# Banded attention and a quantised feed-forward on one core: four score banks in the first half of a batch, and another order of the work around them

## Chip, core and metric

One core of one Trainium2 chip runs the whole program. The metric is the device time of one execution in microseconds; the kernel before took 1425.24 us (median of three). One further execution was taken with the hardware profiler; every duration below is from that one.

## What is computed

Sixteen sequences of 256 tokens with 512 features pass through an attention block against a context of the same shape, and then through a feed-forward block with quantised weights and activations. Cut to what matters:

```
q = rope(layernorm(x) @ wq.T);  k = rope(ctx @ wk.T);  v = ctx @ wv.T      # 16 heads of 32
scores = (q @ k.T) * sqrt(32), only where |query - key| <= 128
attn   = softmax(scores)
x = x + (attn @ v) @ wo.T + wo_b
hidden = gelu(quant16(layernorm(x)) @ quant8(W_in) + b_in)
x = x + quant16(hidden) @ quant8(W_out) + b_out
```

The change lies in the attention block alone.

## The kernel before

**Steps.** The attention block is software-pipelined over the 16 batches. Step b (b = 0 to 15) computes the scores, softmax and weighted sums of batch b, the projections of batch b+1, and what is left of batch b-1 (division by the softmax's denominators, the output projection, the residual). Steps 0 and 1 are written out, steps 2 to 13 are a loop of six rounds with two steps in its body (an even one and an odd one), steps 14 and 15 are written out again. Each engine runs its own list of instructions in the order in which it is written, and waits on semaphores; nothing reorders it. `wait_ge(s, v)` holds an engine, and all that is behind it in its list, until the semaphore has reached v.

**First half of a step.** For each of the 16 heads TensorE (PE) writes a 128x512 block of scores into a PSUM bank (`scores`, L547, two matmuls for a head), and VectorE (DVE) adds the mask and takes the maximum of each row (`row_maxima`, L1002, two instructions for a head). The banks are `ring = bank[0:2]`: head n uses bank n % 2, so head n has to wait until the maxima of head n-2 are taken. After each pair of heads both engines do other work, taken from a table with eight places: `tiles` on PE, `between` on DVE. On PE these are the two tiles of the key projection (`qk_tile(b+1, "k", 0)` and `1`, 24 matmuls each), eight transposes of the normalised x (`x_transposes`, L472), `shares` (below), the two tiles of the query projection, and the two of the value projection (`v_tile`), the second in two pieces. On DVE these are the statistics of the second layernorm (`ln2_moments`, L964 to L984), `invert` (L1044: the reciprocals of the denominators of batch b-1), `largest` (L988), `xt_rest` (L1035: the low part of the transposed x), `rotate` (L1025 to L1028: the rotary embedding, from the banks of the projection), and `normalise` (L1049: batch b-1's weighted sums times the reciprocals).

**How batch b-1's division runs.** The denominators of batch b-1 stand in `den_bank`, which is `q_bank[1]`, at the end of step b-1. `invert` reads them and writes `den_r` (`neg_max` in the rows). `shares` (L482: eight matmuls in the trace with the constant `pick`) spreads the reciprocals over the partitions, into `pv_bank` (banks 6 and 7). `normalise` multiplies. Since x_transposes writes both banks of `q_bank`, it waits for `den_done`, that is, for `invert`. ACT (ScalarE) has by then copied the weighted sums out of `pv_bank` into `oT` (`oT_copy`), so banks 6 and 7 are free from the end of step b-1 on.

**After it.** ACT splits the rotated keys (`split_hi`, L741) and `oT` (`ot_lead`, L772) into high parts, POOL (GpSimd) makes the low parts (L1269, then `ot_rest`, L1280). With these PE starts the second half: the output projection of batch b-1 (`o_products`, L531) is woven into the transposed scores, the exponentials, the weighted sums and the denominators of batch b, and the last matmuls of the step are the transposes of a block of weights (`w_transposes`, L609). The second half uses `ring` with two banks too; the change leaves its order alone.

Of the kernel before, what the change touches and what calls it, by code (L numbers as in the profile page):

```python
# [29 lines left out]
P = 128  # L30
# [50 lines left out]
def build(nc, t):  # L81
# [11 lines left out]
    with ExitStack() as ctx:  # L93
# [90 lines left out]
        ring = bank[0:2]  # L184
        kv_bank = bank[2:4]
# [270 lines left out]
        def _(pe):  # L456
# [7 lines left out]
            def x_transposes(j, s):  # L464

                if s == 0:
                    pe.wait_ge(ln1_norm, 2 * j + 2)
                    wait(pe, wt_done, j - 1)
                    wait(pe, den_done, j - 1)
                    wait(pe, rope_step["q"], ROPE_OPS * j)  # L470
                for c in range(KC):
                    mm = pe.transpose(q_bank[s][:, c * P:(c + 1) * P], x_ln[:, s, c * P:(c + 1) * P], ident[:])  # L472
                mm.then_inc(xt_mm, 1)

            def shares(j):

                for half in range(2):
                    if half == 0:
                        pe.wait_ge(den_done, j + 1)
                    pe.wait_ge(oT_out, 2 * j + half + 1)  # L480
                    for a in range(2):
                        mm = pe.matmul(pv_bank[half][:, a * S:(a + 1) * S], pick[:, 2 * half + a], den_r, start=True, stop=True)  # L482
                    mm.then_inc(share_mm, 1)
# [53 lines left out]
            def scores(b, n):  # L537

                if n % KC == 0:
                    for name in ("k", "q"):  # L540
                        pe.wait_ge(stacked[name][n // KC], STAGED * (b + 1))
                if n < 2:
                    wait(pe, exp_done, H * b)
                else:
                    pe.wait_ge(max_done, 2 * (H * b + n - 1))
                for qb in range(2):
                    mm = pe.matmul(ring[n % 2][:, qb * S:(qb + 1) * S], q_st[0:MROW, n, qb * P:(qb + 1) * P],  # L547
                                   k_st[0:MROW, n], start=True, stop=True)
                mm.then_inc(s_mm, 1)

            def max_transposes(b):

                pe.wait_ge(msplit, 2 * (b + 1))
                wait(pe, onorm, 2 * b)
# [17 lines left out]
            def weighted(b, par, i, kb):  # L572
                if kb == 0:
                    pe.wait_ge(p_ready, 2 * (H * b + KC * (i + 1)))
                    if i == 0:
                        pe.wait_ge(v_done, 2 * (b + 1))
                        wait(pe, onorm, 2 * b)
                    elif i == 2:
                        pe.wait_ge(mT_done, MAX_COPIES * (b + 1))
# [47 lines left out]
            def step(b, par, has_c, has_o, has_proj, has_xt):  # L627

                tiles = [[] for _ in range(H // 2)]
                if has_proj:  # L630
                    tiles[0] += [lambda: qk_tile(b + 1, "k", 0)]
                    tiles[1] += [lambda: x_transposes(b + 1, 0), lambda: x_transposes(b + 1, 1), lambda: qk_tile(b + 1, "k", 1)]
                if has_o:
                    tiles[2] += [lambda: shares(b - 1)]
                if has_proj:
# [325 lines left out]
        def _(dve):  # L961
# [35 lines left out]
            def row_maxima(b, n):  # L997
                dve.wait_ge(s_mm, H * b + n + 1)
                apart(dve)
                for qb in range(2):  # L1000
                    sc = ring[n % 2][:, qb * S:(qb + 1) * S]
# [44 lines left out]
            def normalise(b, half):  # L1046
                dve.wait_ge(share_mm, 2 * b + half + 1)
                part = oT[:, 2 * half:2 * half + 2].rearrange("p i t -> p (i t)")
                dve.tensor_tensor(part, part, pv_bank[half][:], ALU.mult).then_inc(onorm, 1)  # L1049
# [38 lines left out]
            def step(b, par, has_c, has_o, has_proj, has_xt):  # L1088
# [5 lines left out]
                if has_proj:  # L1094
                    between[1] += [lambda: xt_rest(b + 1, 0), lambda: xt_rest(b + 1, 1)]
                    between[2] += [lambda: rotate(b + 1, "k", 0)]
                    between[3] += [lambda: rotate(b + 1, "k", 1)]
                if has_o:
                    between[0] += [lambda: invert(b - 1)]
                    between[4] += [lambda: normalise(b - 1, 0), lambda: normalise(b - 1, 1)]  # L1100
# [299 lines left out]
```

## Time and profile before

| what | us |
|---|---|
| median of three runs | 1425.24 |
| lowest, highest | 1421.88, 1426.4 |
| the profiled execution, its own time | 1428.15 |
| its span | 1426.4 |
| PE busy in the span | 1240.3 (87%) |
| DVE busy in the span | 912.6 (64%) |
| ACT, POOL busy | 692.0 (49%), 454.5 (32%) |

The attention block takes roughly the first 905 us, the feed-forward the rest. Busy shares are means over stages with different limits, so the step must be read in order of time, engine by engine. In the rows a line number such as L547 is the line of the kernel before; "bank<-k_st,q_st" is what an instruction writes and reads; "x4" means that four instructions in a row are merged; what stands in brackets is the time for which the engine stood idle before it, and what ended that.

### The profile page before, as it was taken

What the parts mean: (1) busy time and instruction counts of PE and PEld (TensorE: products, weight loads), DVE (VectorE), ACT (ScalarE), POOL (GpSimd) and SP (SyncE); (2) the same over time, 40 slices, a digit from 0 to 9 for tenths busy, and PEclk for the clock granted to TensorE, in tenths of its full rate; (3) what the DMA queues carried; (4) which work ended last, traced back from release to release, by engine and by line L of the source; (5) the groups of instructions that cost most, each with busy time, mean ns of one, the idle gap of its engine ahead of it and who ended that gap; (6) DMA issues with size and microseconds to landing.
All of it is one profiled execution on the core that took longest, in us unless ns stands there. A gap on an engine that the chain in (4) does not pass through costs nothing.

```text
span 1426.4 us, 26171 instructions
## 1 busy us (share of the span) xinstructions
PE 1240.3 (87%) x7860; PEld 782.0 (55%) x7904; DVE 912.6 (64%) x2359; ACT 692.0 (49%) x1046; POOL 454.5 (32%) x1031
## 2 busy tenths in 40 slices
PE   3689998898898898898898988499999979998888
PEld 3657657657657657657657645344454434433333
DVE  4558558458558468558558654456566658866775
ACT  2243354354354354354354354255556547766664
POOL 2353463463463463463463443100000003111310
PEclk9899999999999999999999997799999989999999
DMA  6432542532542532532532441136555220466664
GB/s 222 119 89 65 145 100 70 143 98 68 144 95 72 142 83 83 144 88 77 144 97 69 115 116 71 66 114 215 196 199 178 83 93 15 139 204 208 192 191 141
DMA packets 88739, 174.54 MB, mean 122 GB/s; under 512 B 12112, under 2 KB 20560, under 8 KB 88656
## 3 DMA queue, kind: packets, MB, share of 16 engines
q1 hardware_dynamic: 74832, 148.45, 35.3%
q10 hardware_dynamic: 13824, 25.17, 6.2%
q8 instruction: 29, 0.48, 0.1%
q14 instruction: 54, 0.44, 0.1%
HBM read 81.30 MB, written 41.94 MB: 86 GB/s over the span
## 4 chain that ended last, share of the span: by engine, by line
PE 36%; issue 27%; DVE 17%; ACT 9%; DMA 7%; POOL 3%; ACTq 1%; DVEq 1%; POOLq 0%; SPq 0%
PE bank L723 7%; DMA h_ring<-hidden_scratch 6%; ACT probs L795 4%; DVE bank L1002 4%; PE bank L568 4%; PE bank L531 4%; PE bank L460 4%; PE bank L461 3%; PE bank L462 3%; PE bank L595 3%; PE bank L582 3%; PE bank L547 3%; ACT q_st L788 2%; DVE row_max L1002 2%; DVE neg_max L1044 2%
## 5 line engine op out<-in xcount | busy, mean ns | idle before, releaser
L1002 DVE CUSTOM_DVE_ANT_0 bank<-bank,mask 128x256 f32<-128x256 f32 x512 | 201.8, 457 | 131.2 <-PE bank L547 100.3
L723 PE MATMUL bank<-wout_int,g_hi 128*128 128x512 bf16 x491 | 186.9, 381 | 24.9 <-DVE g_lo L1247 23.1
L723 PE MATMUL bank<-wout_int,g_lo 128*128 128x512 bf16 x512 | 195.0, 381 | 5.8 <-DVE g_lo L1247 3.0
L692 PE MATMUL bank<-qT_lo,win_int 128*128 128x512 bf16 x512 | 194.0, 379 | 2.8 <-DVE qT_lo L1165 1.6
L692 PE MATMUL bank<-qT_hi,win_int 128*128 128x512 bf16 x489 | 185.4, 379 | 0.0
L795 ACT ACTIVATE probs<-bank 128x512 f32<-128x512 f32 x256 | 144.4, 597 | 61.5 <-PE bank L595 39.7
L568 PE MATMUL bank<-q_st,k_st 128*128 128x256 f32 x512 | 124.2, 326 | 31.2 <-ACT probs L795 24.4
L568 PEld LDWEIGHTS bank<-q_st,k_st 128*128 128x128 f32 x512 | 80.3, 192 | 117.0 <-issue 42.2
L1247 DVE TENSOR_TENSOR g_lo<-h_int,g_hi 128x512 f16<-128x512 f32 x128 | 102.5, 800 | 60.0 <-ACT g_hi L927 58.1
L1305 POOL TENSOR_SCALAR_AFFINE_SELECT probs<-probs 128x128 f32<-128x128 f32 x256 | 82.3, 322 | 150.1 <-ACT probs L795 141.2
L547 PE MATMUL bank<-k_st,q_st 96*128 96x256 f32 x512 | 105.5, 312 | 26.7 <-DVE row_max L1002 14.4
L892 ACT ACTIVATE h_ring<-bank,b_in,g_scale 128x512 f32<-128x512 f32 x96 | 73.5, 780 | 75.1 <-PE bank L692 61.5
L936 ACT ACTIVATE h_int<-h_ring,magic_c,tiny 128x512 f32<-128x512 f32 x96 | 78.4, 817 | 54.9 <-DMA h_ring<-hidden_scratch 44.7
L547 PEld LDWEIGHTS bank<-k_st,q_st 96*128 96x128 f32 x512 | 79.0, 196 | 44.8 <-DVE row_max L1002 23.9
L723 PEld LDWEIGHTS bank<-wout_int,g_hi 128*128 128x128 f16 x512 | 50.2, 98 | 96.8 <-issue 25.8
L1189 DVE TENSOR_REDUCE hmax<-h_ring 128x512 f32 (+1 forms) x96 | 63.4, 683 | 60.5 <-ACT h_ring L892 58.5
L1365 POOL TENSOR_TENSOR xq<-xq,b_out 128x512 f32<-128x512 f32 x32 | 47.0, 1498 | 172.0 <-DMA xq<-x_scratch 164.7
L741 ACT CAST k_hi<-roped 128x1024 fp32r<-128x1024 f32 x16 | 16.8, 1051 | 173.9 <-DVE roped L1028 173.9
L988 DVE TENSOR_REDUCE dmax<-rt 128x512 f32 (+1 forms) x32 | 21.9, 685 | 120.7 <-ACT rt L783 120.7
L582 PE MATMUL bank<-probs,v_sb 128*32 128x256 f32 x1024 | 79.4, 393 | 15.2 <-POOL probs L1307 15.0
L1269 POOL TENSOR_TENSOR k_lo<-roped,k_hi 128x256 fp32r<-128x256 f32 x64 | 45.2, 739 | 145.6 <-ACT k_hi L741 145.6
L1285 POOL TENSOR_TENSOR x_res<-x_res,wo_b 128x512 f32<-128x512 f32 x32 | 40.3, 1280 | 149.4 <-DMA x_res<-in_x 149.4
(146 smaller groups left out, 2948.9 us busy)
## 6 DMA issues: line engine op xcount, KB each, us to landing
hidden_scratch<-h_ring SPq DMA_DIRECT2D x96, 256.0 KB, 2.1
h_ring<-hidden_scratch ACTq DMA_DIRECT2D x96, 256.0 KB, 2.9
k_st<-k_hi SPq DMA_DIRECT2D x128, 128.0 KB, 2.9
q_st<-q_hi SPq DMA_DIRECT2D x128, 128.0 KB, 2.5
xq<-x_scratch SPq DMA_DIRECT2D x16, 1024.0 KB, 6.5
x_ln<-in_x SPq DMA_DIRECT2D x16, 512.0 KB, 3.6
ctx_raw<-in_ctxT SPq DMA_DIRECT2D x16, 512.0 KB, 5.4
k_st<-k_lo SPq DMA_DIRECT2D x64, 128.0 KB, 2.4
```

Source lines behind the costliest of these rows:

```text
L547: mm = pe.matmul(ring[n % 2][:, qb * S:(qb + 1) * S], q_st[0:MROW, n, qb * P:(qb + 1) * P], k_st[0:MROW, n], start=True, stop=True)
L568: mm = pe.matmul(ring[n % 2][:, kb * S:(kb + 1) * S], k_st[:, n, kb * P:(kb + 1) * P], q_st[:, n], start=True, stop=True)
L582: mm = pe.matmul(pv_bank[i // 2][DK * c:DK * (c + 1), (i % 2) * S:(i % 2 + 1) * S], v_sb[:, par, kb, n], probs[:, n % SLOTS, kb], start=kb ...
L692: mm = pe.matmul(bank[f % 4][:], win_int[:, c, f * P:(f + 1) * P], part[:, par, c], start=c == 0 and part is qT_hi, stop=c == KC - 1 and p ...
L723: mm = pe.matmul(bank[4 * par + u][:], part[:, f % 4, u * P:(u + 1) * P], wout_int[:, f], start=f == 0 and part is g_hi, stop=f == FC - 1 ...
L795: act.activation(probs[:, n % SLOTS].rearrange("p k q -> p (k q)"), ring[n % 2][:], ACT.Exp, scale=SCORE_SCALE).then_inc(exp_done, 1)
L892: act.activation(dst, bank[f % 4][:], ACT.Gelu, bias=b_in[:, f:f + 1], scale=g_scale[:, f:f + 1]).then_inc(gelu_done, 1)
L936: act.activation(h_int[:, f % 4], chunk, ACT.Identity, bias=magic_c[:], scale=tiny[:, 5:6]).then_inc(hint_done, 1)
L1002: dve.tensor_tensor_reduce(sc, sc, mask[:, (1 - qb) * P:(1 - qb) * P + S], 1.0, NEG, ALU.add, ALU.max, row_max[:, qb, n:n + 1]).then_inc(m ...
L1189: dve.tensor_reduce(hmax[:, bass.ds(FC * n + f, 1)], src, AX_X, ALU.max, apply_absolute_value=True).then_inc(hmax_done, 1)
L1247: dve.tensor_tensor(g_lo[:, f % 4], h_int[:, f % 4], g_hi[:, f % 4], ALU.subtract).then_inc(glo_done, 1)
L1305: pool.affine_select(out=lower, in_=lower, compare_op=ALU.is_ge, fill=0.0, base=0, pattern=[[-1, P]], channel_multiplier=1).then_inc(p_rea ...
```

## The change

In the first half of a step the scores go through four banks, `ring4 = [bank 0, 1, 6, 7]`: head n uses bank `ring4[n % 4]` and, from head 4 on, waits for the maxima of head n-4 where it waited for those of n-2. Banks 6 and 7 were where `shares` wrote, so `shares` now writes into `q_bank` (banks 4 and 5). There the transposes of x are written too, so these now wait for `normalise` (`onorm`), where they waited for `invert` and the copy of the weights. `shares` stands ahead of the transposes, after heads 2 and 3. The transposes and the second key tile stand one place later, after heads 4 and 5. On DVE `invert` is the first thing in a step, `normalise` comes after head 3, and `xt_rest` and both rotations of the keys stand one place later each.

```diff
+        ring4 = [bank[0], bank[1], bank[6], bank[7]]
...
                 if s == 0:
                     pe.wait_ge(ln1_norm, 2 * j + 2)
-                    wait(pe, wt_done, j - 1)
-                    wait(pe, den_done, j - 1)
+                    wait(pe, onorm, 2 * (j - 1))
                     wait(pe, rope_step["q"], ROPE_OPS * j)
...
             def shares(j):
 
+                pe.wait_ge(wt_done, j + 1)
+                pe.wait_ge(den_done, j + 1)
                 for half in range(2):
-                    if half == 0:
-                        pe.wait_ge(den_done, j + 1)
-                    pe.wait_ge(oT_out, 2 * j + half + 1)
                     for a in range(2):
-                        mm = pe.matmul(pv_bank[half][:, a * S:(a + 1) * S], pick[:, 2 * half + a], den_r, start=True, stop=True)
+                        mm = pe.matmul(q_bank[half][:, a * S:(a + 1) * S], pick[:, 2 * half + a], den_r, start=True, stop=True)
...
+                elif n < 4:
+                    wait(pe, oT_out, 2 * (b - 1) + n - 1)
                 else:
-                    pe.wait_ge(max_done, 2 * (H * b + n - 1))
+                    pe.wait_ge(max_done, 2 * (H * b + n - 3))
...
+                if has_o:
+                    tiles[1] += [lambda: shares(b - 1)]
                 if has_proj:
                     tiles[0] += [lambda: qk_tile(b + 1, "k", 0)]
-                    tiles[1] += [lambda: x_transposes(b + 1, 0), lambda: x_transposes(b + 1, 1), lambda: qk_tile(b + 1, "k", 1)]
-                if has_o:
-                    tiles[2] += [lambda: shares(b - 1)]
-                if has_proj:
+                    tiles[2] += [lambda: x_transposes(b + 1, 0), lambda: x_transposes(b + 1, 1), lambda: qk_tile(b + 1, "k", 1)]
...
             def normalise(b, half):
                 dve.wait_ge(share_mm, 2 * b + half + 1)
+                dve.wait_ge(oT_out, 2 * b + half + 1)
...
-                    between[1] += [lambda: xt_rest(b + 1, 0), lambda: xt_rest(b + 1, 1)]
-                    between[2] += [lambda: rotate(b + 1, "k", 0)]
-                    between[3] += [lambda: rotate(b + 1, "k", 1)]
+                    between[2] += [lambda: xt_rest(b + 1, 0), lambda: xt_rest(b + 1, 1)]
+                    between[3] += [lambda: rotate(b + 1, "k", 0)]
+                    between[4] += [lambda: rotate(b + 1, "k", 1)]
                 if has_o:
-                    between[0] += [lambda: invert(b - 1)]
-                    between[4] += [lambda: normalise(b - 1, 0), lambda: normalise(b - 1, 1)]
+                    between[1] += [lambda: normalise(b - 1, 0), lambda: normalise(b - 1, 1)]
+                    invert(b - 1)
```

Two waits are gone with it: `max_transposes` and the first weighted sums no longer wait for `onorm`.

The first place is PE's list in step 1, from the scores of heads 2 and 3 on (the other odd steps have the same order). Before:

```order
357 L547 MATMUL bank<-k_st,q_st 128x256 [waits max_done]
358 L547 MATMUL bank<-k_st,q_st 128x256
359 L547 MATMUL bank<-k_st,q_st 128x256 [waits max_done]
360 L547 MATMUL bank<-k_st,q_st 128x256
361 L472 MATMUL bank<-ident,x_ln 128x128 [waits den_done,rope_q_step,wt_done,ln1_norm]
362 L472 MATMUL bank<-ident,x_ln 128x128 x7
```

And of the kernel changed, from the same scores on (`neg_max` holds the reciprocals, L481 is `shares`):

```order
354 L548 MATMUL bank<-k_st,q_st 128x256 [waits oT_out]
355 L548 MATMUL bank<-k_st,q_st 128x256
356 L548 MATMUL bank<-k_st,q_st 128x256 [waits oT_out]
357 L548 MATMUL bank<-k_st,q_st 128x256
358 L481 MATMUL bank<-neg_max,pick 128x256 [waits den_done,wt_done]
359 L481 MATMUL bank<-neg_max,pick 128x256 x3
360 L548 MATMUL bank<-k_st,q_st 128x256 [waits max_done,q_stacked1,k_stacked1]
361 L548 MATMUL bank<-k_st,q_st 128x256
362 L548 MATMUL bank<-k_st,q_st 128x256 [waits max_done]
363 L548 MATMUL bank<-k_st,q_st 128x256
364 L472 MATMUL bank<-ident,x_ln 128x128 [waits rope_q_step,onorm,ln1_norm]
365 L472 MATMUL bank<-ident,x_ln 128x128 x7
```

`shares` and the scores of heads 4 and 5 have moved ahead of the transposes, and the transposes wait for `onorm` in place of `den_done`.

The second place is DVE's list in the even step of the loop, from the loop's turn to what PE's transposes wait for. Before, that is the reciprocal:

```order
230 L244 ISA
231 L1002 ISA bank,row_max<-bank,mask 128x256
...
240 L981 ISA
241 L964 BN_STATS bn<-x_res 128x6
...
246 L984 COPY ln_mv<-mv 128x2
...
249 L254 ISA
250 L1044 RECIPROCAL neg_max<-bank 128x256
```

In the kernel changed, it is the second of the two multiplications by the reciprocals (L1048; rows 233 to 242 and 251 to 260 are the maxima of heads 0, 1 and 2, 3):

```order
231 L255 ISA
232 L1042 RECIPROCAL neg_max<-bank 128x256
233 L996 ISA
...
244 L962 BN_STATS bn<-x_res 128x6
...
249 L982 COPY ln_mv<-mv 128x2
...
262 L986 TENSOR_REDUCE dmax<-rt 128x1
263 L1045 REGISTER_ALU
264 L1048 TENSOR_TENSOR oT<-oT,bank 128x512
265 L1045 REGISTER_ALU
266 L1048 TENSOR_TENSOR oT<-oT,bank 128x512
```

Between the start of DVE's step and the release of the transposes there stood the maxima of two heads, the statistics and the reciprocal; now there stand the reciprocal, the maxima of four heads, the statistics, `largest` and both multiplications.

## Rows read from the trace of the kernel before

**Rows 1.** The page's first line: the span of the profiled execution.

```profile
span 1426.4 us, 26171 instructions
```

**Rows 2.** Waits of PE, 55 to 850 us: us in total, times, longest.

```profile
PE bank L472 <- DVE neg_max L1044: 30.1, 13, 4.2
...
PE bank L547 <- DVE row_max L1002: 6.7, 29, 0.9
```

**Rows 3.** PE in step 9: start, us, engine, line, operation, count [idle before].

```profile
534.88 0.40 PE L609 MATMUL bank<-ident_b,w_q 128*128 128x128 bf16 x4
535.08 0.72 PE L547 MATMUL bank<-k_st,q_st 96*128 96x256 f32 x4
...
538.47 0.64 PE L547 MATMUL bank<-k_st,q_st 96*128 96x256 f32 x4
540.64 1.06 PE L472 MATMUL bank<-ident,x_ln 128*128 128x128 f32 x8 [1.54 <-DVE neg_max L1044]
...
544.37 0.64 PE L547 MATMUL bank<-k_st,q_st 96*128 96x256 f32 x4
544.85 1.89 PE L482 MATMUL bank<-neg_max,pick 128*128 128x256 f32 x8
...
554.22 0.50 PE L547 MATMUL bank<-k_st,q_st 96*128 96x256 f32 x2 [0.20 <-DVE row_max L1002]
...
561.39 0.39 PE L531 MATMUL bank<-wo_hi,t_hi 128*128 128x512 f32 x1
```

**Rows 4.** DVE in step 9, the same columns.

```profile
535.76 0.43 DVE L1002 CUSTOM_DVE_ANT_0 bank<-bank,mask 128x256 f32<-128x256 f32 x1 [2.70 <-PE bank L547]
...
537.25 0.69 DVE L964 BATCH_NORM_STATS2 bn<-x_res 128x6 f32<-128x512 f32 x1
...
538.63 1.76 DVE L1044 RECIPROCAL neg_max<-bank 128x256 f32<-128x256 f32 x1
540.31 0.41 DVE L1002 CUSTOM_DVE_ANT_0 bank<-bank,mask 128x256 f32<-128x256 f32 x1
...
541.78 0.69 DVE L988 TENSOR_REDUCE dmax<-rt 128x512 f32 x1
...
544.96 0.43 DVE L1002 CUSTOM_DVE_ANT_0 bank<-bank,mask 128x256 f32<-128x256 f32 x1 [1.30 <-PE bank L547]
...
551.56 0.69 DVE L1028 TENSOR_TENSOR roped<-rt 128x512 f32<-128x512 f32 x1
...
554.02 1.28 DVE L1049 TENSOR_TENSOR oT<-oT,bank 128x512 f32<-128x512 f32 x2
```

**Rows 5.** POOL in step 9, the low parts of the weighted sums.

```profile
556.40 2.54 POOL L1280 TENSOR_TENSOR t_lo<-oT,t_hi 128x512 fp32r<-128x512 f32 x2
```

**Rows 6.** PE in step 10, which follows the loop's turn.

```profile
586.12 0.40 PE L609 MATMUL bank<-ident_b,w_q 128*128 128x128 bf16 x4
...
594.21 1.41 PE L472 MATMUL bank<-ident,x_ln 128*128 128x128 f32 x8 [3.24 <-DVE neg_max L1044]
```

**Rows 7.** DVE in step 10.

```profile
588.78 0.43 DVE L1002 CUSTOM_DVE_ANT_0 bank<-bank,mask 128x256 f32<-128x256 f32 x1 [4.47 <-issue]
...
592.22 1.76 DVE L1044 RECIPROCAL neg_max<-bank 128x256 f32<-128x256 f32 x1 [0.59 <-DVE ln_mv L984]
```

**Rows 8.** PE in steps 2 and 4: transposes, then the first of `shares`.

```profile
164.50 1.76 PE L472 MATMUL bank<-ident,x_ln 128*128 128x128 f32 x8 [2.09 <-DVE neg_max L1044]
...
170.30 1.89 PE L482 MATMUL bank<-neg_max,pick 128*128 128x256 f32 x8
...
271.43 1.97 PE L472 MATMUL bank<-ident,x_ln 128*128 128x128 f32 x8 [3.24 <-DVE neg_max L1044]
...
278.38 0.81 PE L482 MATMUL bank<-neg_max,pick 128*128 128x256 f32 x3
```

**Rows 9.** Stretches: us; busy PE, PEld, DVE, ACT, POOL; granted clock; DMA.

```profile
164.40:166.00 1.60, 1.50 (x9) 1.51 (x9) 1.60 (x9) 0.56 (x1) 0.00 (x0) 0.61 0.00 0
...
540.00:542.00 2.00, 1.35 (x12) 1.39 (x13) 2.00 (x10) 0.69 (x2) 0.00 (x0) 1.00 0.10 39
```

More of the change, by code:

```diff
@@ L543, in scores @@
                     wait(pe, exp_done, H * b)
+                elif n < 4:
+                    wait(pe, oT_out, 2 * (b - 1) + n - 1)
                 else:
-                    pe.wait_ge(max_done, 2 * (H * b + n - 1))
+                    pe.wait_ge(max_done, 2 * (H * b + n - 3))
                 for qb in range(2):
-                    mm = pe.matmul(ring[n % 2][:, qb * S:(qb + 1) * S], q_st[0:MROW, n, qb * P:(qb + 1) * P],
+                    mm = pe.matmul(ring4[n % 4][:, qb * S:(qb + 1) * S], q_st[0:MROW, n, qb * P:(qb + 1) * P],
                                    k_st[0:MROW, n], start=True, stop=True)
@@ L553, in max_transposes @@
                 pe.wait_ge(msplit, 2 * (b + 1))
-                wait(pe, onorm, 2 * b)
                 for qb in range(2):
@@ L576, in weighted @@
                         pe.wait_ge(v_done, 2 * (b + 1))
-                        wait(pe, onorm, 2 * b)
                     elif i == 2:
@@ L1000, in row_maxima @@
                 for qb in range(2):
-                    sc = ring[n % 2][:, qb * S:(qb + 1) * S]
+                    sc = ring4[n % 4][:, qb * S:(qb + 1) * S]
                     dve.tensor_tensor_reduce(sc, sc, mask[:, (1 - qb) * P:(1 - qb) * P + S], 1.0, NEG, ALU.add, ALU.max,
@@ L1047, in normalise @@
                 dve.wait_ge(share_mm, 2 * b + half + 1)
+                dve.wait_ge(oT_out, 2 * b + half + 1)
                 part = oT[:, 2 * half:2 * half + 2].rearrange("p i t -> p (i t)")
-                dve.tensor_tensor(part, part, pv_bank[half][:], ALU.mult).then_inc(onorm, 1)
+                dve.tensor_tensor(part, part, q_bank[half][:], ALU.mult).then_inc(onorm, 1)
             def quantise_win(b):
```

## Prediction

> **What bounds the kernel now.** The span is 1426.4 us [rows 1]; all that the change touches is the attention block, so I read first which waits PE has between 55 and 850 us. Two belong to the first half of a step: the transposes of x wait 30.1 us in all, 13 times, for the reciprocals, and the scores wait 6.7 us, 29 times, for row maxima whose bank they need [rows 2]. So the two-bank ring, which the change doubles, costs little, and the place to look at is what the transposes wait for. Then I read one step in order of time. I call w the start of the weight transposes that end the step before. In step 9, w is 534.88; the transposes start at 540.64 (w + 5.76) after 1.54 us idle, and the output projection, with which the second half opens, at 561.39, 20.75 us behind the transposes [rows 3]. In between PE waits for little (0.20 us before head 11 is such a wait). The even steps of the loop differ in one thing: DVE shows 4.47 us of idle with no releaser before its first maximum, which starts at 588.78, and PE's transposes start at 594.21, that is w + 8.09 [rows 6, 7]. The question is therefore what the change does to two distances: from w to the transposes, and from the transposes to the output projection.
>
> **From w to the transposes, odd steps.** They now wait for the second multiplication (`normalise`), and on DVE there stand ahead of it, each from its start to the next start in [rows 4]: the reciprocal 1.68 (538.63 to 540.31), the maxima of heads 0, 1 1.49 (535.76 to 537.25), the statistics 1.38 (537.25 to 538.63), the maxima of heads 2, 3 1.47 (540.31 to 541.78), `largest` 0.6 (0.69, less some 0.1 by which starts overlap), the multiplications 1.28. That is 7.9. The reciprocal can start when the last denominators are written, which I put at w + 0.2, since PE issues the next scores at 535.08, right behind the weight transposes. From a reciprocal's end (540.39) to the transposes (540.64) it is 0.25. Sum: w + 8.35 where it was w + 5.76, so **2.6 later**. PE's own work does not reach so far: heads 2, 3 are out at w + 4.1 (538.47 and 0.5 for two heads), `shares` adds 1.54 (544.85 until head 6 at 546.39 by the merged group), heads 4, 5 another 0.5: ready at w + 6.1, idle for **2.2 us**. The reciprocals are there by w + 1.9, so `shares` itself waits for nothing; its old cover, the time after the transposes, is given back below.
>
> **From w to the transposes, even steps in the loop (4 to 12, five of them).** The reciprocal now is what DVE has first after the loop's turn. I let it start where the maximum started, at w + 2.66 [rows 6, 7], and add 7.9 and 0.25: w + 10.8, against 8.09, **2.7 later**. In step 10 the statistics took some 0.5 longer than in step 9 (592.22 - 590.28 against 1.38: the first is the reciprocal's start, the second the end of the maxima by the 1.49 above [rows 7]); part of that may stay, so 2.7 to 3.3. `shares` waits here until w + 4.3 or so for the reciprocals, ahead of a longer idle time, at no cost.
>
> **From the transposes to the output projection.** Gone from this stretch are `shares`, heads 4 and 5, and ring waits: 1.54 + 0.5 + some 0.6. New is a wait at the value tile. PE: transposes and second key tile 3.73 (540.64 to 544.37), then twice two heads and a 24-matmul query tile, 3.39 each at most (535.08 to 538.47), then heads 10, 11 for 0.5: ready at 11.0. The value tile overwrites a bank that the second rotation of the keys reads, and this rotation now comes after head 9. DVE: first maximum of head 6 0.59 behind its scores (544.37 to 544.96), so at 4.3; from there two rounds of maxima and rotation are 7.29 (544.96 to 551.56 + 0.69 [rows 4]): 11.6, with the release 11.8. So PE stands 0.8 us there. From the value tile to the output projection it was 561.39 - 554.45 = 6.9 [rows 3], of which 0.2 is a ring wait: 11.8 + 6.7 = **18.5, 2.25 less than 20.75**. POOL runs to the same end: its low parts ended at 558.94, 6.7 behind the rotation's end at 552.25 [rows 4, 5], so now at 18.3 to 18.4. That leaves it 0.1 us of slack where it had 2.4.
>
> **Sum without the clock.** Odd steps 3 to 13 and step 14, which has no turn of the loop ahead of it: 2.6 - 2.25 = +0.35, seven times, 2.5. Even steps: 2.7 to 3.3 less 2.25, +0.6, five times, 3. In steps 0 and 1 some or none of batch b-1's work is there, in step 2 it all is but DVE's late start is not, in step 15 there are no transposes: within 1 us together, by the same counting. **About +5 us.** The four banks let PE run ahead, but what it runs up against is DVE's list, and that list got longer ahead of the release by the maxima of two heads, `largest` and both multiplications.
>
> **The clock.** In step 9, with 1.54 us idle ahead of the transposes, the granted clock is 1.00 (2.4 GHz); in step 2, with 2.09 idle, the stretch from the transposes on shows 0.61 (between 2.4 and 1.2 GHz) [rows 8, 9]. From the transposes to `shares` it took 5.80 us there against 4.21 in step 9 [rows 3, 8], 1.6 more; in step 4, after 3.24 idle, 6.95, 2.7 more [rows 8]. So a fall costs 1.6 to 2.7, and the even steps pay it already. With 2.2 us idle the odd ones are on step 2's side of the two rows: I take six of seven falling at 1.9 (nearer to the low end, where the idle time is nearest): **+11**. Bounds are 0 (none falls) and 19 (seven at 2.7).
>
> Together +16 on a span of 1426.4. The profiled execution took 1428.15 itself, 2.9 above the median of 1425.24; the difference carries over, so the forecast for the median is 1425.2 + 16 = **1441 us**.
>
> The Trainium skill (Perfetto Trace Analysis, Optimizing Tensor Performance, Matmuls) says that independent groups of matmuls should go round through different PSUM banks so that one's evacuation overlaps the next's matmuls. The trace agrees that such waits exist, but prices them at 6.7 us in all [rows 2].
>
> **The rivals.**
> (1) The same chain, but the clock holds in the odd steps, because PE does `shares` and two more heads right before it goes idle. For it: six idle times of 1.54 did no harm. Against: 2.09 did. It gives 1425.2 + 5 = 1430.
> (2) Faster: the 4.47 us of DVE at the loop's turn [rows 7] is not the turn but a delay of the first maximum's own wait. Then the reciprocal starts at w + 0.2 there too, 2.5 sooner than I put it; five times 2.5 is 12.5, and the even steps become odd ones: 1430 - 12.5 = 1417, if the odd ones keep their clock. It decides from the point at which the reciprocal starts before w + 1.5 in steps 4, 6, ... 12. Against it: step 10 and step 9 run the same instructions there, and only the one behind the turn has the idle time.
> (3) The banks pay what the rings cost and the longer list costs nothing, since it runs under PE's run-ahead: 6.7 less, 1418.5. For it, there are 2.25 us per step given back; against, my count of DVE's list, which is 2.6 us longer. The rule of the Trainium skill above would give this one.
> (4) POOL's 0.1 us of slack is not there, and the output projection waits for the low parts of the weighted sums in every step: with 1 us each, 14 more, 1455.
>
> **How the numbers follow.** Forecast with the clock falling in most odd steps 0.57; (1) 0.22; (2) 0.06; (3) 0.05; (4) 0.08; the rest 0.02. The forecast's own bounds are 1435 to 1449 (three to seven falls, low or high price). With (1) it takes in 0.79 from 1427 on, which is the range, opened to 1450. A measurement of this kernel can tell about 0.3%, 4.3 us, from no change. The forecast and (4) are slower by more than that; (1) lies on the border at 1430 and is halved; (2) and (3) are faster. With the rest split: slower 0.76, same 0.13, faster 0.11.
>
> **What would show it.** In the profile after: PE's transposes idle for some 2.2 us in odd and 4 to 5 us in even steps, put down to the multiplication and no longer to the reciprocal; waits of scores for row maxima near zero; a new wait of the value tile for the rotation of 0.8 us; PE's clock in the row of slices lower over the attention block. Wrong would be the whole sum if the transposes started before w + 7.5 in odd steps, the turn's part if the reciprocal started before w + 1.5 in even ones, and the clock's part if transposes to second key tile take 3.7 us in odd steps. The feed-forward must not move.

## The result, and the profile after

| what | before | changed |
|---|---|---|
| median, us | 1422.08 (8 runs) | 1431.47 (8 runs) |
| lowest, highest | 1413.74, 1426.4 | 1430.08, 1437.84 |
| profiled execution, its own time | 1428.15 | 1430.19 |
| its span | 1426.4 | 1428.4 |

The ratio is 1.0081, with a 95% interval of 1.0052 to 1.0109: the change costs 0.8%, 9 to 12 us. On two other chips, where both kernels ran side by side later, it was 1.0038 (1.0011 to 1.0065) and 1.0037 (1.0014 to 1.006), so 0.4 to 0.8% is the size. The change is slower, as forecast, by less than the 16 us of the forecast. The kernel before came out 3.2 us lower over eight executions than over the three from which the forecast of 1441 started.

The waits of PE over the attention block in the changed kernel, which answer to [rows 2]:

```profile
PE bank L568 <- ACT probs L793: 24.3, 45, 1.2
PE bank L472 <- DVE oT L1048: 22.7, 6, 4.2
PE bank L581 <- POOL probs L1306: 15.7, 27, 2.2
PE bank L472 <- issue: 14.1, 8, 1.9
PE bank L548 <- DMA q_st<-q_lo: 10.8, 1, 10.8
PE bank L461 <- DVE roped L1026: 10.5, 15, 0.7
```

The wait for the reciprocals is gone and one for the multiplications (L1048) has come. The trace names it in the even steps; in the odd ones it says "issue", 14.1 us in 8 places, the wait being at the same instruction. Together that is 36.8 us where it was 30.1. The value tile's wait for the rotation of the keys (L1026) is new, 10.5 us in 15 places. The scores' waits for row maxima, 6.7 us before, stand in no row of this list any more. So what the four banks were to remove is gone, and more has come. The feed-forward did not move: from the last weight transposes on it takes 531.4 us, where it took 531.8.

Step 11 of the changed kernel, PE, from w = 641.33 on, the undisturbed odd step (it answers to [rows 3]):

```profile
641.33 0.40 PE L608 MATMUL bank<-ident_b,w_q 128*128 128x128 bf16 x4
641.53 0.72 PE L548 MATMUL bank<-k_st,q_st 96*128 96x256 f32 x4
...
645.39 1.89 PE L481 MATMUL bank<-neg_max,pick 128*128 128x256 f32 x8
...
649.69 1.06 PE L472 MATMUL bank<-ident,x_ln 128*128 128x128 f32 x8 [1.94 <-issue]
...
653.42 0.64 PE L548 MATMUL bank<-k_st,q_st 96*128 96x256 f32 x4
...
661.38 0.50 PE L461 MATMUL bank<-wv_hi,cT_hi 128*128 128x512 f32 x1 [0.72 <-DVE roped L1026]
...
668.21 0.50 PE L530 MATMUL bank<-wo_hi,t_hi 128*128 128x512 f32 x1
```

Transposes at w + 8.36, 1.94 us idle ahead of them; the value tile (L461 with `wv_hi`) waits 0.72; the output projection starts at 668.21, 18.52 behind the transposes. DVE in the same step, which answers to [rows 4]:

```profile
641.46 1.76 DVE L1042 RECIPROCAL neg_max<-bank 128x256 f32<-128x256 f32 x1 [1.95 <-PE bank L594]
643.14 0.41 DVE L1000 CUSTOM_DVE_ANT_0 bank<-bank,mask 128x256 f32<-128x256 f32 x1
...
648.31 1.28 DVE L1048 TENSOR_TENSOR oT<-oT,bank 128x512 f32<-128x512 f32 x2
...
660.63 0.69 DVE L1026 TENSOR_TENSOR roped<-rt 128x512 f32<-128x512 f32 x1
```

The reciprocal starts at w + 0.13; the multiplications start at 648.31 and, 1.38 later, the transposes start. In step 10, the even one, the same places are (PE, then DVE; [rows 6, 7]):

```profile
585.69 0.40 PE L608 MATMUL bank<-ident_b,w_q 128*128 128x128 bf16 x4
...
596.40 1.70 PE L472 MATMUL bank<-ident,x_ln 128*128 128x128 f32 x8 [4.17 <-DVE oT L1048]
```

```profile
587.88 1.76 DVE L1042 RECIPROCAL neg_max<-bank 128x256 f32<-128x256 f32 x1 [4.01 <-issue]
```

w + 10.71 with 4.17 us idle, and the 4.01 us without a releaser at the loop's turn now stand before the reciprocal.

The granted clock, in the columns of [rows 9], in step 9 (transposes at 540.81, which is w + 8.36 too, and 1.94 idle too) and in step 11 (649.69):

```profile
540.80:542.80 2.00, 1.99 (x15) 2.00 (x16) 2.00 (x10) 1.07 (x2) 0.77 (x1) 0.83 0.31 121
542.80:544.80 2.00, 2.00 (x11) 2.00 (x10) 0.60 (x1) 0.00 (x0) 1.75 (x2) 0.50 0.79 260
649.70:651.70 2.00, 2.00 (x18) 2.00 (x19) 2.00 (x10) 1.08 (x2) 0.51 (x1) 1.00 0.45 174
```

Two steps that are alike up to the transposes: in one the clock falls within the first 2 us and then stands at 0.50, that is 1.2 GHz, in the other it holds at 2.4 GHz. From the transposes to the first query tile it is 5.73 us in the one and 4.20 in the other.

### The profile page after: what moved, and what is told of

The parts are those of the page before. It is cut to its first block, busy times and chain, and to the rows that moved or that the text cites. A ratio compares the mean times of both kernels' runs of the same rounds, so it can differ in the third digit from the quotient of the medians.

```text
span 1428.4 us, 26187 instructions
## 1 busy us (share of the span) xinstructions
PE 1229.6 (86%) x7860; PEld 776.5 (54%) x7904; DVE 916.9 (64%) x2359; ACT 688.8 (48%) x1046; POOL 454.9 (32%) x1031
## 4 chain that ended last, share of the span: by engine, by line
PE 39%; issue 28%; DVE 14%; ACT 8%; DMA 7%; POOL 2%; ACTq 1%; DVEq 1%; POOLq 0%; SPq 0%
DMA h_ring<-hidden_scratch 6%; PE bank L721 6%; PE bank L568 4%; PE bank L461 4%; ACT probs L793 4%; PE bank L462 4%; PE bank L463 4%; PE bank L530 4%; PE bank L594 3%; PE bank L581 3%; DVE bank L1000 3%; PE bank L548 3%; ACT q_st L786 2%; DVE roped L1026 2%; PE bank L472 2%
## 5 line engine op out<-in xcount | busy, mean ns | idle before, releaser
L721 PEld LDWEIGHTS bank<-wout_int,g_hi 128*128 128x128 f16 x512 | 50.2, 98 | 96.8 <-issue 21.1
L548 PE MATMUL bank<-k_st,q_st 96*128 96x256 f32 x512 | 89.8, 298 | 14.4 <-DMA q_st<-q_lo 10.8
L461 PE MATMUL bank<-cT_hi,wk_hi 128*128 128x256 f32 x256 | 80.1, 313 | 7.7 <-DVE wk_lo L1074 7.7
```

The lines of the kernel that those rows point to most:

```text
L461: pe.matmul(out, l_hi, r_hi, start=first, stop=False)
L548: mm = pe.matmul(ring4[n % 4][:, qb * S:(qb + 1) * S], q_st[0:MROW, n, qb * P:(qb + 1) * P], k_st[0:MROW, n], start=True, stop=True)
L721: mm = pe.matmul(bank[4 * par + u][:], part[:, f % 4, u * P:(u + 1) * P], wout_int[:, f], start=f == 0 and part is g_hi, stop=f == FC - 1 ...
```

## The experiments

Each kernel but e7 was timed in 5 to 12 executions, beside the kernel before on the same chip. Group 1 ran on one chip; of group 2, e5, e6, e7 and e9 ran on a second, e8 and e10 on a third, e11 and e12 on a fourth. The changed kernel itself was timed beside e10 and e11 alone, so other comparisons with it go by the ratios to the kernel before. "w" is the start of the weight transposes, as ahead. A "fall" is counted where from the transposes to the first query tile it takes 1.3 us or more longer than in an undisturbed step: 4.2 in the changed order, 6.4 in the order of the kernel before, where `shares` and two more heads lie in between; "odd steps" are 3 to 13 and 14, seven in all, "even" ones 4 to 12, five in all.

### Group 1: what the transposes wait for

**e1_invert_first.** The kernel before, with one line moved:

```diff
                 if has_o:
-                    between[0] += [lambda: invert(b - 1)]
                     between[4] += [lambda: normalise(b - 1, 0), lambda: normalise(b - 1, 1)]
+                if has_o:
+                    invert(b - 1)
                 for n in range(H):
                     row_maxima(b, n)
```

> The kernel before with one part of the change alone: the reciprocal of batch b-1's denominators is the first thing VectorE does in a step; two score banks, shares in banks 6 and 7, and PE's order stay. Theory (what PE's transposes wait for decides, not the score banks): the reciprocals are there at w + 1.9 in odd steps (0.2 + 1.7), before PE gets to the transposes, so these start at w + 4.1 where it was w + 5.76, 1.65 less in steps 3 to 14 that are odd or 14; in the even steps of the loop they start at w + 4.5 where it was 8.1 to 9.4, and the clock no longer falls. There VectorE is late by its turn of the loop and gives part back as waits for row maxima: 3.5 to 4 less per step. Sum 7 x 1.65 + 6 x 3.8 = 34 us less than before, about 1388. Rival (VectorE's list bounds the first half, so what is moved in it comes back as waits of scores and tiles for it): under 12 us less.

Measured: 1394.88 us, ratio to before 0.9831 (0.9799 to 0.9864), 24 us less. The transposes start at w + 4.07 in odd steps and w + 4.9 to 6.6 in even ones, with no wait, and no step shows a fall. But 24 us is between the two theories. One reason is in its waits:

```profile
PE bank L547 <- DVE row_max L1002: 24.5, 55, 1.8
```

The scores now wait 24.5 us for row maxima: once the long wait is gone, the two banks do bind, and the output projection comes at w + 25.0 to 25.9 in odd steps and not at w + 24.9. The seven odd steps together save 7.7 us where 11.6 were forecast. The even ones save 4.0 each in the profiled execution, as forecast, and its span is 37 us below that of the first profile of the kernel before; but this execution, 1390.76, was the second fastest of six that go up to 1402.2, and what the slower ones lost no trace shows. The transposes' wait for the reciprocals was worth a lot; the banks are what is late next.

**e2_largest_late, e3_norm_first, e4_largest_twice.** The changed kernel with VectorE's list ahead of the multiplications 0.6 us shorter, shorter by the statistics too, and 0.6 us longer.

```diff
# e2
-                    between[1] += [lambda: largest(b - 2, 1)]
+                    between[2] += [lambda: largest(b - 2, 1)]
# e3, besides e2's
-                    between[0] += [lambda: ln2_moments(b - 2, 1)]
...
                     between[1] += [lambda: normalise(b - 1, 0), lambda: normalise(b - 1, 1)]
+                    if has_c:
+                        between[1] += [lambda: ln2_moments(b - 2, 1)]
# e4, in largest(j, 1), ahead of the reduction
+                    dve.tensor_reduce(tiny[:, 7:8], rt[:, s].rearrange("p c t -> p (c t)"), AX_X, ALU.max,
+                                      apply_absolute_value=True)
```

> The changed kernel with one VectorE instruction moved: the absolute maximum of the second layernorm's input (largest, 0.6 us) stands behind the maxima of heads 4 and 5 and no longer ahead of the two multiplications. Theory (the length of VectorE's list ahead of the release): transposes at w + 7.76 in odd steps, idle before them 1.35 us, clock falls in none of them; 0.6 less in 13 steps and two falls of 1.5 less: 11 us less than the changed kernel. Rival (the list length does not matter, the price of the change is the new wait of the value tile for the keys' rotation, 0.7 us a step): no difference, the transposes' earlier start comes back as a longer wait there.

> The changed kernel with the second layernorm's statistics moved behind the two multiplications and its absolute maximum behind the maxima of heads 4 and 5. Theory: the multiplications now wait for shares and follow the maxima of heads 2 and 3 at once; transposes at w + 7.2 in odd steps and w + 8.4 in even ones (10.2 to 11.4 in the changed kernel), idle 0.8 and 2.0. VectorE reaches the rest of the transposed x 0.5 later relative to the transposes, so a query tile waits 0.5. Sum 7 x 0.7 + 6 x 2 + 3 for two falls of the clock: 20 us less than the changed kernel. Rival (the value tile's wait for the rotation sets the end): no more than e2 gives.

> The changed kernel with the absolute maximum ahead of the multiplications done twice (0.6 us more; the first result goes to an unused cell). Theory: transposes at w + 8.96 in odd steps, idle 2.5; each of 13 steps 0.6 longer, and the clock falls in the odd steps that kept it too (five more at 1.5 to 2.7): 16 to 21 us more than the changed kernel. If the clock does not follow the idle time: 8 us more.

| kernel | median, us | ratio to before | transposes, odd steps | idle before them | falls, odd | falls, even |
|---|---|---|---|---|---|---|
| e3 | 1399.06 | 0.9861 (0.9835 to 0.9887) | w + 7.07 | 0.64 | 0 | 0 |
| e2 | 1417.74 | 0.9969 (0.9943 to 0.9994) | w + 7.77 | 1.35 | 0 of 7 | 5 of 5 |
| changed | 1431.47 | 1.0081 (1.0052 to 1.0109) | w + 8.36 | 1.94 | 2 of 7 | 5 of 5 |
| e4 | 1444.47 | 1.0168 (1.0141 to 1.0195) | w + 8.96 | 2.53 | 3 of 7 | 5 of 5 |

The rows of the transposes in an odd step of e3, e2 and e4 (step 11 in each; w is 616.73, 637.46 and 654.14), one fence for each:

```profile
623.80 1.06 PE L472 MATMUL bank<-ident,x_ln 128*128 128x128 f32 x8 [0.64 <-issue]
```

```profile
645.23 1.06 PE L472 MATMUL bank<-ident,x_ln 128*128 128x128 f32 x8 [1.35 <-issue]
```

```profile
663.10 1.06 PE L472 MATMUL bank<-ident,x_ln 128*128 128x128 f32 x8 [2.53 <-issue]
```

(The row "changed" was timed on another chip.) In e2 and e4 the start of the transposes follows the length of VectorE's list to 0.1 us, in both directions, and the time follows the start. In e3 it follows it only in part: the list is 1.4 us shorter than e2's, the start comes 0.7 earlier. VectorE now stands idle for TensorE's scores of head 2 ahead of the multiplications:

```profile
620.92 0.43 DVE L1000 CUSTOM_DVE_ANT_0 bank<-bank,mask 128x256 f32<-128x256 f32 x1 [0.77 <-PE bank L548]
```

The rival of e2, that an earlier start comes back as a longer wait of the value tile, falls: that wait stayed at 0.7. e3's value tile waits 0.3 and its query tile 0.6, and it still gains 31 us on the changed kernel by the ratios (20 were expected; e2 gained 16 for 11, e4 lost 12 for 16 to 21; ratios measured on different chips are good to some 6 us, as will be seen). e3's forecast left out that the even steps would keep their clock too: with 1.73 to 1.92 us idle ahead of the transposes none of the five fell. What failed in e4's expectation is the clock: with 2.53 us idle (2.71 in step 14) only three of seven odd steps fell, so longer idle time did not make the fall certain.

### Group 2: the banks, the clock, and a better version

**e5_two_banks, e10_four_held, and both compared with the changed kernel on one chip.** e5 is the changed kernel with two banks, e10 with four banks but the waits of two.

```diff
# e5
-        ring4 = [bank[0], bank[1], bank[6], bank[7]]
+        ring4 = [bank[0], bank[1], bank[0], bank[1]]
...
-                    pe.wait_ge(max_done, 2 * (H * b + n - 3))
+                    pe.wait_ge(max_done, 2 * (H * b + n - 1))
# e10: the second of the two edits, for every head from 2 on
```

> The changed kernel with its four score banks taken back to two; shares stays in banks 4 and 5, and both orders stay. Theory (in the changed order the banks do nothing, since VectorE's list releases the transposes and the value tile): scores of heads 4 and 5 wait for maxima, but PE is ahead of its release there by 1.9 us; 0 to 0.3 us a step, 0 to 4 us more than the changed kernel. Rival (the four banks carry a gain that the changed order eats up): 7 us or more above the changed kernel.

Measured: 1425.83, ratio 1.0017 (0.9996 to 1.0039). Against the changed kernel's 1.0081 that was 9 us less with two banks than with four, which neither theory had. Its profile, of its fastest execution (1417.59), offered a reason: with two banks the idle time ahead of the transposes lies in pieces (scores of heads 4 and 5 each wait), and four of five even steps did not fall. So a new theory was formed, that running ahead gathers idle time and thereby costs the clock, and e10 was to test it; e8_after_again, the changed kernel, ran beside it.

> The changed kernel, unchanged, on the same chip as e10_four_held, as its measure. It should come out 0.5 to 1.1% above the kernel before, as at first, with every even step and two or three odd ones slow from the transposes to the query tile (5.7 us or more where 4.2 is the undisturbed length).

> The changed kernel with its four banks kept, but every head made to wait as with two banks, for the maxima of head n-2. It came out that two banks (e5_two_banks) are faster than four, 1.0017 against 1.0081 of before. Theory (running ahead on PE gathers its idle time into one piece before the transposes, and there the clock falls; with two banks the same idle time lies in four pieces between scores): this kernel is like e5, 0.9995 to 1.004 of before, transposes still start at w + 8.36 in odd steps, idle 1.3 before them, and the even steps take 4.2 from the transposes to the query tile in most cases. Rival (banks 6 and 7 as such cost something, or e5 was a chip's difference): it stays with the changed kernel, 1.005 to 1.011.

Measured on that chip: the changed kernel 1431.46, ratio 1.0038 (1.0011 to 1.0065), less than the 0.5 to 1.1% expected of it; e10 1431.66, ratio 1.0032 (1.0009 to 1.0056). e10 lies in the range that the theory gave for it, but so does the changed kernel beside it: no difference, and the theory falls as far as the time goes. Its other half came true: three of e10's five even steps kept their clock. The last two runs put e5's edit beside the changed kernel:

> e5_two_banks once more, beside the changed kernel on one chip, since the two were only compared through the kernel before on different chips, and e10_four_held, which waits as e5 does with four banks, came out at the changed kernel's time. If e5's advantage was a chip's difference (what e10 says), the two differ by under 3 us; if two banks are really faster than four in this order, it is 5 to 9 us ahead.

> The changed kernel beside e11_two_again on one chip. 1.004 to 1.008 of before; by the first reading 3 us or less from e11_two_again, by the second 5 to 9 us above it.

Measured: two banks 1430.17, ratio 1.0027 (1.0007 to 1.0047); four banks 1432.01, ratio 1.0037 (1.0014 to 1.006). Most of the 9 us came from comparing across chips: two banks gave 1.0017 and 1.0027, the changed kernel 1.0081 where it was first measured and 1.0038 and 1.0037 later. Side by side on one chip, running ahead gains nothing. The medians differ by 0 and 2 us; the means of the changed kernel are 2 us higher both times, with an uncertainty of some 3 us each, so a small loss is possible and not shown. That banks do next to nothing here is what e5's first theory said. A ratio taken on one chip and compared with one from another is thus uncertain by more than its interval.

**Falls of the clock in three executions of the changed kernel.** The profiled executions of the changed kernel, of e8 and of e12 are the same program. Odd steps with a fall: 2, 1 and 6 of 7. Even steps: 5 of 5 in each. Their spans are 1428.4, 1429.2 and 1435.5. In the kernel before, profiled twice, it is 0 of 7 in both, and 5 of 5. Its step 2, on which the prediction's line for the clock rests [rows 8, 9], is another matter: it fell after 2.09 us idle in the first profile and held after 2.08 in the second (e7), with 6.43 us from the transposes to the query tile and a granted clock of 1.00:

```profile
159.60:161.60 2.00, 1.94 (x17) 1.95 (x18) 2.00 (x10) 1.07 (x2) 0.00 (x0) 1.00 0.35 61
```

Step 2 of the changed kernel does the same: it fell after 2.41 and 2.32 us and held after 2.31.

Pieces of idle time did not protect the odd steps: e10 has three falls in them, e5 one and e11 two, with 1.27 to 1.28 us idle before the transposes and a wait of 0.20 to 0.26 before that. In even steps fewer fell: in these three profiles 4 of 15, where it was 15 of 15 in the three of the changed kernel, and the five even steps took 271 to 277 us together where they took 280 to 286. The timed medians do not show these 3 to 15 us; why, no run here says. Two stretches of e10's step 9, from the transposes at 541.12 on:

```profile
541.10:543.10 2.00, 1.98 (x14) 2.00 (x15) 2.00 (x10) 1.07 (x2) 0.52 (x1) 0.77 0.46 178
543.10:545.10 2.00, 2.00 (x12) 2.00 (x11) 0.60 (x2) 0.00 (x0) 2.00 (x2) 0.50 0.81 241
```

The granted clock falls within the first stretch (0.77 is its mean) and is at the lower of its two levels in the second, though no single wait ahead of it was as long as the 1.35 us after which e2 kept the higher one.

**e6_fill_idle.** The changed kernel, with matmuls that nobody reads in the idle time:

```diff
+            def fill(j, count):
+
+                pe.wait_ge(res_done, 2 * (j - 2))
+                for m in range(count):
+                    c = m % KC
+                    pe.matmul(kv_bank[1][:, 0:S], w_hi["wk"][:, c, 0:P], cT_hi[:, c], start=c == 0, stop=c == KC - 1)
...
+                        tiles[2] += [lambda: fill(b + 1, 12 if par else 32)]
```

> The changed kernel with extra matmuls of 128x256 on PE ahead of the transposes of x, 12 in odd steps and 32 in even ones from step 2 on, into bank 3, which the second key tile overwrites; 12 take 1.4 us and 32 take 3.8 us. They fill the idle time and move nothing else. Theory (the clock's fall comes from that idle time and costs 1.5 to 2.7 each): transposes start where they did, w + 8.4 and w + 10.2 to 11.4, and no step takes more than 3.8 us from the transposes to head 6; two odd and six even falls are gone, 10 to 15 us less than the changed kernel. Rival (the clock falls for the transposes themselves or for what the whole core does): no difference; 0 to 3 us more where VectorE's loop turn comes early and the filling is the longer.

Measured: 1431.86, ratio 1.007 (1.0045 to 1.0095), beside 1.0081, 1.0038 and 1.0037 of the changed kernel on other chips: no gain that can be told. The trace, of the fastest of its eight executions (1425.51), shows both halves of that. In its step 10 (w = 584.69):

```profile
590.38 0.83 PE L555 MATMUL bank<-k_st,q_st 96*128 96x256 f32 x4
591.05 3.93 PE L500 MATMUL bank<-cT_hi,wk_hi 128*128 128x256 f32 x32
595.38 1.09 PE L472 MATMUL bank<-ident,x_ln 128*128 128x128 f32 x8 [0.39 <-DVE oT L1057]
...
599.13 0.64 PE L555 MATMUL bank<-k_st,q_st 96*128 96x256 f32 x4
```

No step of e6 shows a fall (4.2 us from the transposes to the query tile in all 14), and from the transposes to the output projection its steps 4, 6, 10 and 12 take 18.5 us where the changed kernel's take 20.1, 20.9, 20.1 and 21.1. That is the clock's price by itself: 1.5 us in an odd step, 1.6 to 2.6 in an even one. But the filling was too long in steps 2 and 14 (transposes at w + 10.05, where they were at 8.74 and 8.29), and PE's longer list had a cost that was not expected, at a turn of the loop:

```profile
471.63 0.40 PE L615 MATMUL bank<-ident_b,w_q 128*128 128x128 bf16 x4
477.34 1.22 PE L555 MATMUL bank<-k_st,q_st 96*128 96x256 f32 x4 [5.31 <-issue]
```

5.31 us without a releaser, on PE, where the changed kernel has none at any turn; that step took 61.4 us, 6.3 more than the same step of the changed kernel. So the fall's price is shown, while the time of the whole says nothing for or against it.

**e9_four_late.** The version that the runs point to: e1, with the multiplications moved up and four banks from head 8 on, when banks 6 and 7 are no longer needed by `shares`.

```diff
+        late = [bank[6], bank[7], bank[0], bank[1]]
...
+            def score_bank(n):
+                return ring[n % 2] if n < 8 else late[n % 4]
...
+                elif n < 10:
+                    if has_o and n == 8:
+                        pe.wait_ge(onorm, 2 * b)
+                else:
+                    pe.wait_ge(max_done, 2 * (H * b + n - 3))
...
-                    between[4] += [lambda: normalise(b - 1, 0), lambda: normalise(b - 1, 1)]
+                    between[2] += [lambda: normalise(b - 1, 0), lambda: normalise(b - 1, 1)]
```

> The version that the first four runs point to: the kernel before with the reciprocal first on VectorE (e1_invert_first), normalise moved from after head 9 to after head 5, and four score banks from head 8 on, when banks 6 and 7 are free of shares. In e1 the scores wait 24.5 us for row maxima, most of it at heads 8 to 11. Theory: with them in four banks the value tile waits for the rotation alone, at w + 17.4 in odd steps (18.2 to 19.0 in e1), the output projection starts at w + 24.1 (25.0 to 25.9): 1 to 1.5 less a step, 15 to 20 us less than e1, 40 to 45 less than before. Rival (VectorE's list is full in the first half, and normalise in front of the rotations takes back what the banks give): within 5 us of e1.

Measured: 1381.28 us, ratio 0.9692 (0.9661 to 0.9724), 44 us less than before and, by the ratios, 20 less than e1: as expected. PE in its step 11 (w = 608.01):

```profile
608.01 0.40 PE L618 MATMUL bank<-ident_b,w_q 128*128 128x128 bf16 x4
...
612.07 1.04 PE L473 MATMUL bank<-ident,x_ln 128*128 128x128 f32 x8
...
624.59 0.64 PE L556 MATMUL bank<-k_st,q_st 96*128 96x256 f32 x4
...
631.72 0.50 PE L532 MATMUL bank<-wo_hi,t_hi 128*128 128x512 f32 x1
```

Transposes at w + 4.06, output projection at w + 23.71, no wait in a bracket between them. In even steps heads 2 and 3, which still have two banks, wait for row maxima behind the turn (1.0 to 2.4 us for head 2), and steps 6 and 8 show a fall with no idle time right before the transposes. This kernel is faster than both others.

**e7_before_again.** The kernel before, profiled once more.

> The kernel before, unchanged, profiled once more, to see how its steps differ from one execution to another. Theory (what an odd step takes is fixed, an even one varies with VectorE's loop turn and with how long the clock stays down): odd steps the same within 0.1 us, transposes at w + 5.76; even ones between 54 and 57.5 us each, with the whole time between 1414 and 1427. Rival (the odd steps also lose the clock in some executions): odd steps of 51.2 and of 52.8 side by side.

Measured: 1422.08, span 1420.3. Odd steps 51.16 to 51.20 us each but for step 3 (51.75) and step 14 (50.11), as in the first profile within 0.1; even ones 53.85 to 57.86, where 54 to 57.5 were expected. The theory held but for the edges of that range.

## Why the prediction was right, and where it was off

**The number.** 1431.47 lies in the range of 1427 to 1450, but below the bounds of 1435 to 1449 that the forecast's own mechanism had; it is in the range because this had been opened down to take in rival (1), whose 1430 is nearer than the forecast's 1441. The direction and the chain were right, the size was not: of the 16 us, 9 to 12 came on this chip and 5 on two others.

**From w to the transposes.** Forecast w + 8.35, measured w + 8.36 in odd steps; in even ones 10.8 to 11.4 was forecast and 10.18 to 11.42 came. That it fits to 0.01 is in part luck: the statistics took 1.61 us where 1.38 was counted, while the reciprocal started 0.07 earlier and the release came 0.10 behind the multiplications where 0.25 was counted. e2 and e4 show that it is the length of this list that releases the transposes; e3 shows how far that goes: with 1.4 us more off the list the start came only 0.7 earlier, since VectorE then waits for TensorE's scores. TensorE was ready at w + 6.4 and not at 6.1, so its idle time was 1.94 and not 2.2.

**The turn of the loop.** The reciprocal was put at w + 2.66, where the first maximum had started; it came at w + 1.66 to 2.90 in the profiled execution and at up to 3.67 in e8. Rival (2) falls: the idle time belongs to the turn, whatever instruction follows it. It differs from one turn to the next by more than a microsecond, and so do the even steps.

**From the transposes to the output projection.** Forecast 18.5, measured 18.52; the value tile's wait was 0.8 and came out at 0.72. Here too two small errors cancel: the tile came 11.69 us behind the transposes (11.8), and from there it was 6.83 us and not 6.7, since the ring wait of 0.20 that the prediction took off this stretch stands ahead of the tile [rows 3]. POOL's end did not hold the output projection up (6.83 us from the value tile on, as in step 9 before), so rival (4) falls; its slack was as narrow as computed, since its last low part ends at 668.02, 0.19 ahead of the projection. The last row of the timeline of POOL in step 11 of the changed kernel (start, duration):

```profile
665.47 2.55 POOL L1279 TENSOR_TENSOR t_lo<-oT,t_hi 128x512 fp32r<-128x512 f32 x2
```

**The sum without the clock.** Seven odd steps were to cost 2.5 us: in the profiled execution they take 363.65 us together against 358.14, 5.5 more, of which two falls are 3.1, and 2.4 is left. The five even ones were to cost 3: they take 279.8 us against 279.6, and 285.7 and 279.9 in the two later profiles, 2.2 more in the mean. So +5 was about right, though the even steps differ by more than this from one execution to the next.

**The clock.** This is the term that was mis-sized. Six falls in seven odd steps at 1.9 us, 11 us, were forecast; three executions show 2, 1 and 6 of them, and the price in an odd step is 1.5. That is 1.5 to 9 us, 4.6 in the mean, and with the +5 it gives some 10, where 5 to 12 were measured on three chips. By the prediction's own sign, 3.7 us from the transposes to the second key tile's end, this part was wrong in five of seven odd steps of the profiled execution (3.73), and the row of PEclk in the page, which was to be lower over the attention block, is the same digit for digit before and after. The reasoning drew one line between two rows, 1.54 and 2.09 us of idle time [rows 3, 8], and treated what lies above it as all but certain. The row above the line was itself one draw: the same step of the same kernel held its clock in e7. The runs show a chance and no such line: with 1.35 no odd step fell in e2, with 1.94 from one to six of seven did, with 2.53 three of seven. The low bound of the term, which was 0, was the better end to be near to. Rival (1), that the clock holds, was nearer: its 1430 is 5 above the median it started from, and two of three chips gave 5. Its mechanism is not shown either, since with the same `shares` and heads before the idle time the clock did fall in some steps.

**The banks.** That the four banks bring next to nothing in this order is confirmed by e10 and e11 beside the changed kernel: the medians differ by 0 and 2 us. Rival (3) falls. What the Trainium skill says of rotating PSUM banks (Perfetto Trace Analysis, Optimizing Tensor Performance, Matmuls) is true of the waits, which went away, and brought no time here, where another release is later. In e9 the banks and the earlier multiplications together brought 20 us by ratios from two chips. What this experiment does not separate is how much of the 20 belongs to either.

**Left open.** What decides whether the clock falls in a given step: two executions of one program differ in the number of falls by five, with the same idle time ahead of each. Why the even steps' kept clock in e5, e10 and e11 does not show in their medians. And whether chips differ by 0.4% in what they make of the same two kernels, or executions scatter more than the intervals say.

## What to carry to other kernels

Before giving a waiting engine more room to run ahead, count the list of the engine that it waits for, from that engine's start to the instruction that releases: here two more banks let TensorE arrive two microseconds before a release that had been moved 2.6 us back. A short instruction that others wait for belongs at the head of its engine's list, ahead of work with slack; that alone gave 1.7%, and with it in place more banks and earlier multiplications gave another 1.4% together, by ratios from two chips. And a buffer that is freed by a late step takes that step's place in the chain: when `shares` moved into the banks of the transposes, the transposes began to wait for VectorE's two multiplications, and with them for all that stands ahead of them.

## What the runs showed of the hardware

The granted clock after an idle time of 1.9 us differed between equal steps: 1, 2 or 6 of 7 at the lower level in three executions of one program, with the same idle time ahead (1.86 to 2.03 us). After 1.7 to 1.9 us the clock held in five of five even steps of e3. At the turn of this loop DVE stands idle for 3.00 to 5.55 us without a releaser (3.00 in e1, 4.47 in [rows 7], 4.01 above, 5.55 in e6; in odd steps of the changed kernel, with no turn, it waits 1.95 there for the denominators). The figure differs by more than 1 us from turn to turn, and TensorE, which had shown none at a turn, had one of 5.31 once 44 matmuls had been added to the loop's body (e6, one turn; what in the longer body costs that was not tried).

Of the turn, the Trainium skill (Runtime: NRT & Kernel Launch, Instruction fetch mechanics) says that a taken branch to a place outside the instructions an engine holds makes it fetch them before it goes on. The rows agree that time without a releaser stands at the turn; that it is this fetch is an explanation that no run here tested.
